# Down products of batches two to four with half-precision operands, in a unit bounded on the chip

## The reference

```python
x = x + attn(layernorm(x), W_q, W_kv, W_o)
x = x + ffn(layernorm(x), gate_w, up_w, down_w, gate_scale, up_scale, down_scale)

def attn(x, W_q, W_kv, W_o):                 # 16 heads of 32 features
    qf  = unit(fft(x @ W_q.T))               # each head's spectrum divided by its norm
    kvf = cumsum(unit(fft(x @ W_kv.T)), axis=tokens)
    return ifft(qf * kvf).real @ W_o.T

def ffn(x, ...):                             # inner width 1536; weights rounded to float8_e4m3
    gate = silu((x @ fp8(gate_w)) * gate_scale)
    up   = (x @ fp8(up_w)) * up_scale
    return ((gate * up) @ fp8(down_w)) * down_scale
```

## Time and profile before

| | us |
|---|---|
| median of 3 runs | 422.19 (420.83 to 422.36) |
| the profiled execution, its own time | 422.29 |
| its span, first to last instruction | 420.4 |
| TensorE busy in the span | 411.4 (98%) |
| VectorE busy | 281.6 (67%) |
| ScalarE busy | 193.2 (46%) |
| GpSimd busy | 102.7 (24%) |
| granted TensorE clock, mean | 0.998 of full speed |

### The profile page before, as it was taken

The page is one execution under the profiler, slowest core; times in us unless marked ns, Lnnn a source line. Parts: engine busy times, 40 slices in busy tenths (PEclk is TensorE's granted clock), DMA queues, the critical chain, the costliest instruction groups (busy, mean ns, idle before and its releaser), DMA issues.

```text
span 420.4 us, 5467 instructions
## 1 busy us (share of the span) xinstructions
PE 411.4 (98%) x1895; PEld 218.9 (52%) x1895; DVE 281.6 (67%) x497; ACT 193.2 (46%) x322; POOL 102.7 (24%) x108
## 2 busy tenths in 40 slices
PE   8999999999999999999999999999999999999994
PEld 4744444455555554554554564454555555555553
DVE  5999998999999695187685953176774744322234
ACT  3687656576746245436322573255342522132220
POOL 0133641014244222045450031043441001300003
PEclk9999999999999999999999999999999999999999
DMA  8996648700271133241112025320112051200002
GB/s 259 272 244 238 176 101 163 164 2 0 62 241 26 30 73 77 49 150 49 27 27 50 2 50 89 63 80 22 25 28 51 0 89 32 80 2 0 2 0 100
DMA packets 57546, 33.54 MB, mean 80 GB/s; under 512 B 49456, under 2 KB 49840, under 8 KB 57392
## 3 DMA queue, kind: packets, MB, share of 16 engines
q1 hardware_dynamic: 57088, 32.93, 31.1%
q10 hardware_dynamic: 432, 0.28, 0.2%
HBM read 17.44 MB, written 4.19 MB: 51 GB/s over the span
## 4 chain that ended last, share of the span: by engine, by line
PE 82%; DMA 4%; DVE 4%; SPq 3%; ACT 3%; POOL 1%; issue 1%; POOLq 0%; DVEq 0%
PE bd L449 20%; PE bg L433 20%; PE bu L433 20%; PE ba L350 10%; PE ba L390 7%; SPq L1606 2%; PE bd L350 2%; PE ba L363 1%; DMA h<-x_dram 1%; DMA hT<-w_q_dram 1%; DMA xT<-xs 1%; POOL xs L1495 1%; PE bd L336 1%; ACT half L708 1%; DMA hT<-ks 1%
## 5 line engine op out<-in xcount | busy, mean ns | idle before, releaser
L449 PE MATMUL bd<-dw,fu 128*128 128x512 f32 x376 | 100.0, 411 | 0.0
L433 PE MATMUL bg<-hT,gu 128*128 128x512 f16 x384 | 91.0, 380 | 0.9 <-DMA hT<-ks 0.9
L433 PE MATMUL bu<-hT,gu 128*128 128x512 f16 x384 | 90.7, 379 | 0.0
L449 PEld LDWEIGHTS bd<-dw,fu 128*128 128x128 f32 x376 | 70.6, 188 | 18.6 <-DVE fu L1152 0.7
L1147 DVE SCALAR_TENSOR_TENSOR ff<-bu,us,sl 128x512 f32<-128x512 f32 x48 | 35.9, 748 | 65.6 <-PE bu L433 62.4
L695 ACT ACTIVATE sl<-bg,gs 128x512 f32<-128x512 f32 x48 | 33.0, 687 | 80.5 <-PE bg L433 79.6
L350 PE MATMUL ba<-wf,xT 128*128 128x512 f16 x288 | 63.2, 379 | 0.0
L433 PEld LDWEIGHTS bu<-hT,gu 128*128 128x128 f16 x384 | 37.6, 98 | 45.3
L433 PEld LDWEIGHTS bg<-hT,gu 128*128 128x128 f16 x384 | 34.9, 98 | 47.5 <-issue 9.8
L1152 DVE TENSOR_TENSOR fu<-ff,fu 128x512 fp32r<-128x512 f32 x47 | 40.1, 854 | 15.7 <-ACT fu L701 15.3
L1521 POOL TENSOR_TENSOR h<-ff,h 128x512 f32<-128x512 f32 x14 | 17.6, 1276 | 129.8 <-DVE ff L1173 129.8
(11 more groups left out here) (178 smaller groups left out, 447.9 us busy)
## 6 DMA issues: line engine op xcount, KB each, us to landing
h<-x_dram SPq DMA_DIRECT2D x16, 256.0 KB, 4.2
out_dram<-h SPq DMA_DIRECT2D x15, 256.0 KB, 2.0
hT<-w_q_dram SPq DMA_DIRECT2D x4, 256.0 KB, 4.2
gu<-w_kv_dram SPq DMA_DIRECT2D x4, 256.0 KB, 4.0
hT<-gate_w_dram SPq DMA_DIRECT2D x2, 512.0 KB, 3.7
hT<-up_w_dram SPq DMA_DIRECT2D x2, 512.0 KB, 6.0
gu<-woT_dram SPq DMA_DIRECT2D x1, 1024.0 KB, 5.5
hT<-down_w_dram SPq DMA_DIRECT2D x2, 512.0 KB, 4.8
```

The source lines that it names most:

```text
L433: m = e.matmul(bk[:, :], gu[:, c, 4 * w + k, col:col + P], hT[:, b % 2, part, k, :], start=k == 0 and part == 0, stop=k == KT - 1 and part ...
L449: m = e.matmul(bd[t][:, :], fu_at(n)[:, part, P * t:P * t + P], dw[:, i, :], start=i == 0 and part == 0, stop=i == NI - 1 and part == 1)
```

## The change

**Operands.** For n of 12 and more, both operands of the down product are half precision (F16). The rounded down weights are copied once by ACT (`act_dw`, 12 copies of 128x512) into `dw16`, which lies over the staging room `own`; `fu_at(n)` now is one of four half-precision slots in `zT`, which batch 0's attention has left. `act_fu` of block n so waits for the down product of block n - 4. Batch 0 (n below 12) stays as it was.

**The unit.** So that the gated products fit into half precision, the up scale of batches 1 to 3 is divided by a bound and the down scale multiplied by it (`us2`, `ds2`). The bound is computed on the chip: POOL adds up the `half` buffers of the 12 gate and up pieces into `peak` (one 128x1024 addition each), and `act_half` of piece n + 4 waits for it. DVE reduces it (`dve_peak`), TensorE turns it over the partitions with two small products (`pe_peak`), DVE combines them (`dve_peak_all`), TensorE spreads the number (`pe_bound`), and DVE scales `us` and `ds` (`dve_bound`).

**Order.** The lists of all five engines are written anew. The staging rooms of the pieces from number 11 on are dealt out differently, so that `own` is free early.

```diff
-STAGE = (..., ("n1", 0), ("n1", 1), ("n1", 0), ("n1", 1), ("e", 0), ("e", 1), ("e", 2))
+STAGE = (..., ("e", 0), ("e", 1), ("e", 2), ("n1", 0), ("n1", 1), ("n1", 0), ("n1", 1))
...
         def fu_at(n):
-            return pT[:, :, :] if n == NB * NI - 1 else fu[:, n % 2, :, :]
+            return fu[:, n % 2, :, :] if n < NI else zT[:, n % 4, :, :]
...
+        def pe_peak(e):
+            vacant(e, ("bound", 0))
+            e.wait_ge(v_top, 3)
+            e.wait_ge(d_id, 16)
+            for n in range(2):
+                m = e.matmul(ba[AT["bound", 0]][0:1, P * n:P * n + P], top[:, n:n + 1], ident, start=True, stop=True)
+            m.then_inc(s_bound, 1)
+
+        def pe_bound(e):
+            vacant(e, ("bound", 1))
+            e.wait_ge(v_peak, 4)
+            e.matmul(ba[AT["bound", 1]][:, 0:1], ones[0:1, :], top[0:1, 3:4], start=True, stop=True).then_inc(s_bound, 1)
...
+            if b == 1 and t == 0:
+                e.wait_ge(a_dw, i + 1)
             for part in range(2):
-                m = e.matmul(bd[t][:, :], fu_at(n)[:, part, P * t:P * t + P], dw[:, i, :],
+                m = e.matmul(bd[t][:, :], fu_at(n)[:, part, P * t:P * t + P], (dw if b == 0 else dw16)[:, i, :],
...
         def act_fu(e, n):
             e.wait_ge(v_f, n + 1)
-            if 1 < n < NB * NI - 1:
+            if 1 < n < NI:
                 e.wait_ge(s_d, 4 * (n - 1))
+            elif NI <= n < NI + 4:
+                e.wait_ge(s_o, 4)
+            elif n > NI:
+                e.wait_ge(s_d, 4 * (n - 3))
...
+                if (n - 4) % 3 < 2:
+                    e.wait_ge(*peaked(n - 4))
             e.activation(part_at(half, n), stage_at(n), ACT.Abs, scale=0.5, saturate=False).then_inc(a_half, 1)
...
+        def act_dw(e, i):
+            e.wait_ge(*rounded(max(13, 3 * (i // 2) + 2)))
+            e.activation(dw16[:, i, :], dw[:, i, :].bitcast(F32), ACT.Copy).then_inc(a_dw, 1)
...
+        def dve_peak(e):
+            e.wait_ge(p_peak, 13)
+            e.wait_ge(d_sc, 48)
+            e.tensor_reduce(top[:, 0:1], peak[:, :], AX.X, ALU.max).then_inc(v_top, 1)
+            e.tensor_tensor(top[:, 4:16], gs[:, :], us[:, :], ALU.mult).then_inc(v_top, 1)
+            e.wait_ge(v_top, 2)
+            e.tensor_reduce(top[:, 1:2], top[:, 4:16], AX.X, ALU.max, apply_absolute_value=True).then_inc(v_top, 1)
...
+        def dve_bound(e):
+            e.wait_ge(s_bound, 2)
+            e.tensor_scalar(top[:, 0:1], ba[AT["bound", 1]][:, 0:1], 4.0 * D * D / 2.0 ** 15, None, ALU.mult).then_inc(v_bound, 2)
...
+            e.tensor_scalar(us2[:, :], us[:, :], top[:, 1:2], None, ALU.mult).then_inc(v_bound, 1)
+            e.tensor_scalar(ds2[:, :], ds[:, :], top[:, 0:1], None, ALU.mult).then_inc(v_bound, 1)
...
+            if n == NI:
+                e.wait_ge(v_bound, 4)
...
+        def pool_peak(e, n):
+            e.wait_ge(*halved(n))
+            e.wait_ge(p_peak, peaked(n)[1] - 1)
+            e.tensor_tensor(peak[:, :], peak[:, :], half[:, n % 4, :], ALU.add).then_inc(p_peak, 1)
...
         def tensor_program(e):
             pe_warm(e, 14)
+            pe_warm(e, 3)
             pe_heads(e, 0, 0)
-            pe_warm(e, 3)
...
             for b in range(1, NB):
...
                     pe_qk(e, nxt, 0, 1)
+                pe_down(e, b * NI - 1)
```

More of the change, by code:

```diff
@@ L73, in tenancies @@
         order += [("o", b, 3)]
+        if b == 1:
+            order += [("bound", 0), ("bound", 1)]
     at, before, last = {}, {}, {}
@@ L169, in build @@
         v_half = sem("dve_half")
+        s_bound, a_dw, v_top, v_peak, v_bound, p_peak = (
+            sem(n) for n in ("pe_bound", "act_dw", "dve_top", "dve_peak", "dve_bound", "pool_peak"))
         v_f, v_fu, v_y, v_out, v_near, v_rd = (
@@ L230, in emptied @@
             kind, *at = piece
+            if kind == "bound":
+                return (v_peak, 2) if at[0] == 0 else (v_bound, 2)
             if kind == "size":
@@ L750, in scalar_program @@
             act_sum_w(e, 1)
+            act_root0(e, 0, [1])
+            act_sum_w(e, 3)
             act_xh(e, 0, 0)
[L752 to L753 removed]
             act_sum_w(e, 5)
@@ L857, in scalar_program @@
+            act_dw(e, 0)
+            act_dw(e, 1)
+            act_dw(e, 2)
+            act_fu(e, 6)
+            act_half(e, 15)
             act_silu(e, 7)
-            act_half(e, 13)
-            act_fu(e, 6)
-            act_half(e, 14)
+            act_ks(e, 1, 3)
+            act_dw(e, 3)
             act_fu(e, 7)
-            act_half(e, 15)
-            act_zh(e, 1, 1)
-            act_row(e, 1, 2)
             act_silu(e, 8)
-            act_fu(e, 8)
+            act_zh(e, 1, 2)
             act_half(e, 16)
@@ L881, in scalar_program @@
-            act_hT(e, 1, 0)
-            act_hT(e, 1, 1)
-            act_hT(e, 1, 2)
+            act_dw(e, 4)
+            act_dw(e, 5)
+            act_xh(e, 2, 0)
+            act_xh(e, 2, 1)
+            act_dw(e, 6)
+            act_fu(e, 10)
+            act_dw(e, 7)
+            act_silu(e, 11)
+            act_sqrt2(e, 1, range(NT))
+            act_dw(e, 8)
+            act_dw(e, 9)
+            act_hT(e, 1, 0)
+            act_dw(e, 10)
+            act_hT(e, 1, 1)
+            act_fu(e, 11)
@@ L1160, in dve_scale_out @@
         def dve_scale_out(e, b, t):
+            by = ds if b == 0 else ds2
+            if b == 1 and t == 0:
+                e.wait_ge(v_bound, 5)
             e.wait_ge(s_d, d_done(NI * b + NI - 1, t))
@@ L1347, in vector_program @@
-            dve_product(e, 1, 3)
-            dve_zl(e, 1, 2)
+            dve_fu(e, 7)
+            dve_round(e, 15)
+            dve_product(e, 1, 3)
+            dve_f(e, 8)
+            dve_zl(e, 1, 2)
+            dve_round(e, 16)
+            dve_o(e, 1, 1)
+            dve_zl(e, 1, 3)
+            dve_f(e, 9)
+            dve_root0_tail(e, 2, range(NT))
+            dve_fu(e, 8)
+            dve_xn(e, 2, 0)
+            dve_round(e, 17)
             dve_f(e, 10)
+            dve_xn(e, 2, 1)
@@ L1601, in sp_hT @@
             elif b == 1:
-                e.wait_ge(*rounded(14))
+                e.wait_ge(*rounded(17))
             else:
```

664 lines of the change are left out of this document (346 added, 318 removed).

## The result

| | median, us | lowest to highest | profiled execution, span |
|---|---|---|---|
| before | 422.36 | 420.83 to 423.97 | 422.29, 420.4 |
| changed | 425.34 | 423.59 to 426.11 | 426.11, 424.3 |

The ratio is 1.0065, with a 95% interval of 1.0039 to 1.0092: the changed kernel is about 2.8 us slower. The prediction was 419.8 and at most 423.2; it was wrong in size and in direction.

A forecast was written before the change was run, and what follows sets the result against it. TensorE's summed work was taken as the bound (busy 411.4 of 420.4 us). Profiled 422.29 - 3.6 (down products) - 0.7 (`fu` waits) + 0.5 (small products) + 0.5 (start) + 0.8 (VectorE waits) = 419.8 us, range 417.9 to 423.2.

The forecast's parts named there:

- The down products: Down groups of batches 1 to 3: half precision takes 1.735 us instead of 1.84, 3.6 us less over 36 groups.
- The waits for `fu`: TensorE's two waits of about 0.36 us before the second block's down product in batches 1 and 2 go: 0.7 us less.
- The small products: New float32 products `pe_peak` and `pe_bound` on TensorE: 0.5 us more, 0.3 if weight loads hide, 0.9 without overlap.
- The wait for VectorE that I placed there: End of batch 0, at `pe_peak`, `pe_bound` and block 11's down product: 0.8 us of new TensorE waits, bounds 0 to 4.
- The start: First projection: constants load later, behind 512 KB more, so it starts 0.5 us later; bounds -0.5 to 2.
- The batch in steady state: Sign in the changed profile: time between the starts of two projection runs falls from 96.86 to 95.3 us.
- VectorE in batch 0: From 82 to 156 us: 3.2 us added plus 2.6 us of stretching fit into 6.45 us idle; 0.8 us of waits.
- A rate of 0.23: Batch 0: GpSimd work stretches VectorE by about 5.4 us per 23.77 us, applied to the new peaks as 2.6 us.
- Rival C: Peaks hold VectorE for their whole length: 8.3 us of TensorE waits from 82 to 160 us, 427.3 us; chance 0.07.
- The count of five peaks after 82 us: Five GpSimd peaks of 2.3 us stand behind batch 1's first addition in its list, so after 82 us.
- Two roundings have been moved ahead of 82 us: VectorE's load from 82 to 156 us is eased by two roundings done earlier; no size given.
- the transposes of hT: Before the first gate block: new issue order could remove their 0.9 us wait or double waits (0 to 2.6 us); left unchanged.

The follow-up runs named there:

- old_half: Kernel before in its own order, with only half-precision down operands in batches 1 to 3 and the fixed unit kept: 420.32 us against 422.73, ratio 0.9935.
- lab: Kernel before with eight VectorE forms, each against one GpSimd peak, added behind its last output; read for those rows only, e.g. rounding 1.23 us alone, 3.00 behind a peak.
- old_memset: Whole change in the order of the kernel before, each of the 12 peaks replaced by a GpSimd write that reads nothing: 426.1 us, ratio 1.0084.
- new_plain: Changed kernel in its new order without the unit bounded on the chip, the fixed unit of before in its place: 426.0 us, ratio 1.0078.
- new_both: Changed kernel with VectorE steps reordered at 41 us (three) and 103 us (two): 423.41 us, ratio 1.0027.

## Why the prediction was wrong

**The down products: right.** -3.6 forecast; 3 x 1.2 = 3.5 us by old_half's batches, and 0.0065 x 422.7 = 2.7 us (1.7 to 3.8) by its runs. A group takes 1.73 us as forecast, batch 0's 1.86 to 1.87.

**The waits for `fu`: right in the new order only.** -0.7 forecast. In the changed kernel both are gone, in old_half both stand, so the four slots alone don't take them away.

**The small products: the term was mis-sized.** 0.5 us forecast with bounds of 0.3 and 0.9, 1.3 measured. The instructions take what the rows gave (0.60 us and 0.38); the weight loads on both sides of them idle for 0.23 to 0.37 us each, which no row of a long run shows. The wait for VectorE that I placed there (+0.8) didn't come.

**The start: wrong, without weight.** +0.5 us forecast, and the first projection is 0.07 us earlier; the text named that as a way to err.

**The batch in steady state.** 95.3 us forecast, 95.90 measured. In it TensorE waits once for ks (0.21 us), and the weight load of the gate block behind it idles 0.58 us for ScalarE; old_half has such waits for ks too, and 95.67. What else is missing I have not taken apart.

**VectorE in batch 0: the step that failed.** It had three faults. The first is the rate. "A rate of 0.23" was an average over all forms and overlaps, and I set it against the Trainium skill's rule as if the rule were an extreme. lab and old_memset show that there is no rate: of the eight forms tried four are held to the end of the peak and four not at all. The 1.38 us of the earlier trace rows against 0.54 alone fits a held instruction. Rival C had the mechanism, but not where it costs: in the old order the unit costs 17.5 us, more than twice its 8.3, and in the changed kernel, whose 425.3 lies near C's 427.3, almost nothing of the loss is such a hold. That C's time is near is luck. The count of five peaks after 82 us is short by one; in the trace six run there.

The second is where that cost is paid. In the changed kernel the peaks hold little. Its roundings average 1295 ns, as they do in new_plain without any peak, because most of its peaks run beside statistics, reductions and reads of PSUM. VectorE and GpSimd of the changed kernel in order of time:

```profile
59.38 0.69 DVE L1170 BATCH_NORM_STATS2 bst<-h 128x6 f32<-128x512 f32 x1
...
60.20 0.66 DVE L1142 TENSOR_TENSOR zT<-ba,zT 128x512 f16<-128x512 f32 x1
...
143.76 2.25 DVE L1160 TENSOR_TENSOR ks<-qk,ks 128x512 f16<-128x512 f32 x1 [0.71 <-ACT ks L710]
```

```profile
58.67 2.01 POOL L1588 TENSOR_TENSOR peak<-peak,half 128x1024 f16<-128x1024 f16 x1
...
134.10 3.08 POOL L1588 TENSOR_TENSOR peak<-peak,half 128x1024 f16<-128x1024 f16 x1
...
140.24 5.23 POOL L1588 TENSOR_TENSOR peak<-peak,half 128x1024 f16<-128x1024 f16 x2
```

The peak at 134.10 is held itself, by a rounding that began at 134.08 (3.08 us instead of 2.01), and so is the one at 140.24; the one behind it holds the subtraction at 143.76 for 2.25 us instead of 0.68, the one long hold of VectorE in this trace. The new order with the unit takes 425.34 us and without it 426.0; the old order takes 437.83 with it and 420.3 without. So the new order takes away nearly all of the 17.5 us that the unit costs in the old one, and costs 5.7 us of its own.

The third fault is the one that decided the sum: **the moved steps were costed at nothing.** "Two roundings have been moved ahead of 82 us" stands in the text as relief for VectorE, with no term for what the setup pays. The sum has one term ahead of the first gate block, +0.5 for the constants; the transposes of hT among others in SP's queue were named with 0 to 2.6 us and put at nothing. What the runs show in its place is the 5.7 us of new_plain over old_half. In the changed kernel's trace 3.6 us of lateness stand ahead of the first gate block: 1.9 by tile 3, with the late copies of wf, and the rest by the copies of wo, which stand behind ScalarE's second square root, at 44.13 instead of 40.36. The prediction read the stretch from 82 to 156 us, where VectorE is nearly full, and none from 20 to 82, where it is as full (in the kernel before, 57.22 of these 62 us are busy).

With the operands at -2.4 us by old_half's median, what is left for order and unit together is +5.0 (422.7 - 2.4 + 5.0 = 425.3); that is a remainder and no measurement of its own. **What stays open** is which moves make up the 5 us, and how much of them the unit would still cost in an order without the waits at wo and at xT. Two neighbouring swaps gave back 1.9 (new_both), within what the intervals leave open; a setup in the old order with the new one behind it made waits of its own.

## What to carry over

Before you add work to GpSimd beside a busy VectorE, list VectorE's forms: in this kernel those with two on-chip tiles in, the clamp and the scaling are held for all of what is left of the GpSimd instruction, those with an input in PSUM, statistics and reductions not at all, and the price hangs on which of them is begun behind it. When a change re-lays the order of four engines to find that room, cost the order itself, in the stretch where the moved steps land, and not the added instructions only. Part a change by factors (operands, unit, order) before you look for single waits: two kernels (old_half and new_plain) told here what no wait did, and a transfer's wait of 1.9 us in one trace was worth 0.2 us in the medians.

## What the runs showed of the hardware

A GpSimd addition of 1024 half-precision and fp8 elements takes 2.00 us, and holds a VectorE instruction of 0.54 to 1.23 us for up to 1.8 us; a GpSimd write of the same bytes takes 1.80 and holds the clamp but not the rounding (lab, old_memset). A small float32 product (or a pair of them) beside a down group costs TensorE 0.6 to 0.7 us. A weight load in fp32r takes 188 ns and one in half precision 98 in both kernels (means of the groups), while the matmul groups differ by only 0.13 us in 1.86. In new_plain a wait of TensorE of 2.0 us was followed by a granted clock of 0.75 over the next 7 us, 1.7 us more on top. A transfer of 2 KB, issued behind three loads of 512 KB, landed after 3.9 to 6.3 us in five traces; in the kernel before, where none stood ahead, one landed after 1.6.
